# First layer: the scores of both token halves in one group on four row groups of TensorE, and a new order of the step

## What is computed

```python
def _block(x, shifted, n1g, n1b, qkvw, qkvb, pw, pb, rpb, n2g, n2b, f1w, f1b, f2w, f2b):
    shortcut = x
    x = _ln(x, n1g, n1b).reshape(B, H, W, DIM)
    if shifted:
        x = jnp.roll(x, (-SHIFT, -SHIFT), (1, 2))
    xw = _win_part(x)
    qkv = (xw @ qkvw.T + qkvb).reshape(-1, N, 3, HEADS, HD).transpose(2, 0, 3, 1, 4)
    q, k, v = (qkv[0], qkv[1], qkv[2])
    attn = jnp.einsum('bhnd,bhmd->bhnm', q * SCALE, k)
    attn = attn + rpb[RPI].transpose(2, 0, 1)[None]
    ...
    attn = jax.nn.softmax(attn, -1)
    xw = jnp.einsum('bhnm,bhmd->bnhd', attn, v).reshape(-1, N, DIM)
    xw = xw @ pw.T + pb
    ...
    h = _ln(x, n2g, n2b)
    h = jax.nn.gelu(h @ f1w.T + f1b, approximate=False) @ f2w.T + f2b
    return x + h
```

## Time and profile before

| what | value |
|---|---|
| median of the runs | 979.84 us |
| the profiled execution | 981.16 us |
| its span on the core | 979.3 us |
| PE busy (matmul), share of the span | 801.5 us, 82% |
| DVE busy | 794.5 us, 81% |
| ACT busy | 574.2 us, 59% |
| POOL busy | 237.1 us, 24% |
| the chain that ended last, by engine | PE 62%, DVE 27%, ACT 5%, issue 3% |
| 302.58 to 313.73 (one step): PE, DVE, ACT busy | 11.15, 9.78, 8.56 us |
| granted clock of TensorE, 17.6 to 52.0 and 302.58 to 313.73 | 0.65 and 1.00 |

### The profile page before, as it was taken

How to read it: one execution, slowest core, us unless ns; L and a number is a source line. 1 busy time by engine, 2 the same in 40 slices (tenths; PEclk the granted TensorE clock), 3 DMA queues, 4 the chain that set the end, 5 groups by cost and what they waited for, 6 DMA issues and landing times.

```text
span 979.3 us, 20396 instructions
## 1 busy us (share of the span) xinstructions
PE 801.5 (82%) x7980; PEld 534.8 (55%) x7980; DVE 794.5 (81%) x2001; ACT 574.2 (59%) x859; POOL 237.1 (24%) x272
## 2 busy tenths in 40 slices
PE   3799999999999999999999988799577668332366
PEld 1577877877787777777777764374211111000053
DVE  8788889988888998888899965755539999899942
ACT  1276777777777777777676663224466664645032
POOL 6122222222222222222222211382201221222021
PEclk8699999999999999999999997889676655565657
DMA  8200000000000000002000000100003665666301
GB/s 229 63 1 3 1 2 2 2 2 2 2 2 2 2 2 1 2 1 105 1 3 2 2 2 1 48 1 1 1 1 66 129 130 102 124 130 129 65 0 33
DMA packets 11621, 34.13 MB, mean 35 GB/s; under 512 B 1879, under 2 KB 4359, under 8 KB 11271
## 3 DMA queue, kind: packets, MB, share of 16 engines
q0 software_dynamic: 5904, 21.24, 11.5%
q1 hardware_dynamic: 5623, 11.60, 4.0%
HBM read 10.81 MB, written 0.79 MB: 12 GB/s over the span
## 4 chain that ended last, share of the span: by engine, by line
PE 62%; DVE 27%; ACT 5%; issue 3%; POOL 1%; DMA 1%; POOLq 0%; SPq 0%; DVEq 0%; ACTq 0%
PE narrow L1450 5%; PE wide L1373 4%; PE scores_a L1422 4%; PE scores_b L1422 4%; DVE prod L989 4%; PE last L1527 4%; DVE prod L997 3%; PE scores_a L1409 3%; PE scores_b L1433 3%; PE scores_b L1409 3%; PE scores_a L1433 3%; PE narrow L1480 3%; PE last L1523 2%; PE wide L1513 2%; PE last L1500 2%
## 5 line engine op out<-in xcount | busy, mean ns | idle before, releaser
L380 POOL TENSOR_TENSOR stb<-stb,neg_half 128x4 f32<-128x4 f32 x48 | 48.4, 1008 | 253.3 <-DVE stb L681 253.3
L1102 ACT ACTIVATE d<-d 128x768 f32<-128x768 f32 x96 | 80.6, 840 | 18.4 <-DVE d L628 17.9
L1450 PEld LDWEIGHTS narrow<-v,pt 128*64 128x64 f32 x2304 | 79.5, 139 | 13.4 <-issue 13.4
L1450 PE MATMUL narrow<-v,pt 128*64 128x54 f32 x2304 | 85.8, 225 | 0.1
L1697 PE MATMUL scores_b<-xb,gates_w 128*32 128x512 bf16 x192 | 26.0, 557 | 60.1 <-DVE yo L1009 51.4
L375 POOL TENSOR_TENSOR sta<-sta,neg_half 128x4 f32<-128x4 f32 x48 | 48.9, 1018 | 104.9 <-DVE sta L568 104.9
L1109 ACT ACTIVATE pt<-scores_a 128x768 f32<-128x768 f32 x48 | 38.9, 810 | 56.7 <-PE scores_a L1433 56.7
L1118 ACT ACT_TABLE_LOAD x47 | 60.3, 1283 | 0.8
L615 DVE TENSOR_REDUCE mx<-scores_a 128x12 f32<-128x768 f32 x48 | 46.0, 958 | 16.8 <-PE scores_a L1422 16.8
L1102 ACT ACT_TABLE_LOAD x46 | 59.0, 1283 | 0.8
L1118 ACT ACTIVATE ga<-wide 128x512 f32<-128x512 f32 x48 | 28.7, 598 | 49.6 <-PE wide L1513 49.5
(11 more groups left out here) (351 smaller groups left out, 2200.9 us busy)
## 6 DMA issues: line engine op xcount, KB each, us to landing
gsum<-mag POOLq DMA_DIRECT2D x14, 512.0 KB, 4.6
ysum<-yo POOLq DMA_DIRECT2D x7, 768.0 KB, 5.8
ysum<-xd POOLq DMA_DIRECT2D x6, 768.0 KB, 5.8
gsum<-mag POOLq DMA_DIRECT2D x14, 256.0 KB, 4.7
wts<-in_wpack SPq DMA_DIRECT2D x6, 442.0 KB, 6.7
sed_w<-in_sed_in SPq DMA_DIRECT2D x1, 2304.0 KB, 8.0
graw<-in_gates_in SPq DMA_DIRECT2D x1, 1152.0 KB, 5.1
x_all<-in_x_tok SPq DMA_DIRECT2D x8, 96.0 KB, 3.2
```

Source lines behind the costliest of these rows:

```text
L1102: act.activation(d, d, ACT.Exp).then_inc(p_ready[u], 1)
L1450: op = pe.matmul(y_ps[64 * b:64 * b + 64, q * VO:(q + 1) * VO], t.pt[:, q, h, 64 * b:64 * b + 64], t.v[:, q, b, h * VO:(h + 1) * VO], star ...
```

## The change

- `scores` takes no half any more: one call does both, after the same waits, and the order inside is v, b, r, u, so that neighbouring matmuls go to different row groups. One semaphore `pe_S` replaces two.
- The order in PE's, DVE's, ACT's and POOL's loops is new. In PE's a slot is now transposed (`windows_T`) in step n, projected and scored in n + 1, its probabilities and values in n + 2, its projection and `fc1_a` in n + 3, `fc1_b` and `fc2` in n + 4. Both `bias` calls stand together, right ahead of `windows_T` and `scores`.
- PE's and ACT's loops run one step longer, DVE's and POOL's two. The jobs tied to fixed steps at the end move by one or two steps with it.
- `gelu` is split into `gelu_a` and `gelu_b`, which stand a step apart; `gelu_b` comes first in a step, then both affine steps, then `gelu_a`.
- Waits follow the new order: `windows_T` waits for `take_v` of the slot before, `project_v` for `add_proj`, `transpose_z` for `affine_a` three slots ahead, each of them the latest reader of the bank y.

```diff
-            for k in range(SLOTS + 4):
-                if k >= 45:
-                    rstd_f(k - 45)
-                rstd_b(k - 3)
-                add_b2(k - 3)
+            for k in range(SLOTS + 6):
+                if k >= 47:
+                    rstd_f(k - 47)
+                add_b2(k - 5)
                 rstd_a(k)
                 if k == 0:
                     rstd_e(1)
                     set_values()
                     rstd_e(2)
+                rstd_b(k - 4)
...
-                        dve.wait_ge(pe_S[1], n - 1)
+                        dve.wait_ge(pe_S, n - 1)
...
-                if r == 0:
-                    dve.wait_ge(mx_ready[u], n + 1)
-                    if n >= 2:
-                        dve.wait_ge(pe_PT[1], n - 1)
+                dve.wait_ge(mx_ready[u], n + 1)
+                if n >= 2:
+                    dve.wait_ge(pe_PT[1], n - 1)
...
-            for k in range(SLOTS + 4):
-                if k >= 45:
-                    final_stats(k - 45)
-                if k == 51:
+            for k in range(SLOTS + 6):
+                if k >= 47:
+                    final_stats(k - 47)
+                if k == 53:
                     fill(4)
                     final_normal(6)
                     fill(5)
-                invert(k - 3)
-                divide(k - 3)
-                subtract(k - 2, 0, 1)
-                take_o(k - 3)
                 if k == 1:
-                    embed_centre(1)
-                normal_a(k - 1)
-                if k == 1:
+                    normal_a(0)
                     embed_square(1)
                     embed_centre(2)
                     embed_square(2)
-                add_proj(k - 3)
-                squares_b(k - 3)
-                variance_b(k - 3)
-                maxima(k - 2, 1)
-                subtract(k - 2, 1, 0)
-                subtract(k - 2, 1, 1)
-                normal_b(k - 3)
-                if k == 50:
+                    embed_finish(1)
+                squares_a(k)
+                normal_b(k - 5)
+                variance_a(k)
+                if k > 1:
+                    normal_a(k - 1)
+                maxima(k - 3, 0)
+                subtract(k - 3, 0, 1)
+                subtract(k - 3, 0, 0)
+                maxima(k - 3, 1)
+                add_mlp(k - 6)
+                subtract(k - 3, 1, 1)
+                invert(k - 4)
+                divide(k - 4)
+                subtract(k - 3, 1, 0)
+                if k == 52:
                     fill(2)
                     fill(3)
-                if k == 2:
+                take_o(k - 4)
+                take_k(k - 2)
+                add_proj(k - 4)
+                squares_b(k - 4)
+                variance_b(k - 4)
+                if k == 3:
                     dve.wait_ge(set_v, 9)
                     dve.wait_ge(set_on, 6)
-                take_v(k - 2)
-                take_k(k - 1)
-                if k == 1:
-                    embed_finish(1)
-                squares_a(k)
-                variance_a(k)
-                add_mlp(k - 4)
-                maxima(k - 1, 0)
-                subtract(k - 1, 0, 0)
-                if 45 <= k < 51:
-                    final_normal(k - 45)
+                take_v(k - 3)
+                if k == 0:
+                    embed_centre(1)
+                if 47 <= k < 53:
+                    final_normal(k - 47)
...
-            def gelu(n):
+            def gelu_a(n):
                 if live(n):
                     t = st[n % 2]
                     act.wait_ge(pe_f1a, n + 1)
                     if n >= 2:
                         act.wait_ge(pe_f2, n - 1)
                     act.activation(t.g1[:], hid_bank[:, :, 0:256], ACT.Gelu).then_inc(g1_made, 1)
+
+            def gelu_b(n):
+                if live(n):
+                    t = st[n % 2]
                     act.wait_ge(pe_f1b, n + 1)
+                    if n >= 2:
+                        act.wait_ge(pe_f2, n - 1)
                     act.activation(t.g2[:], z_ps[:, 0:256], ACT.Gelu).then_inc(g2_made, 1)
 
...
-            for k in range(SLOTS + 3):
+            for k in range(SLOTS + 4):
+                exponential(k - 2, 0)
+                take_q(k - 1)
+                exponential(k - 2, 1)
                 take_PT(k - 2, 0)
-                exponential(k - 2, 1)
-                take_q(k - 1)
-                affine_b(k - 3)
-                if k == 50:
-                    fill(3)
                 take_PT(k - 2, 1)
-                gelu(k - 3)
-                exponential(k - 1, 0)
+                gelu_b(k - 4)
                 affine_a(k)
                 if k % CHUNKS == 1 and k // CHUNKS < BLOCKS - 1:
                     table_high(k // CHUNKS + 1)
                 if k % CHUNKS == 4 and k // CHUNKS < BLOCKS - 1:
                     table_middle(k // CHUNKS + 1)
-                if k == 49:
+                affine_b(k - 3)
+                if k == 50:
                     for c in range(3):
                         fill(c)
+                gelu_a(k - 3)
                 if k == 50:
+                    fill(3)
+                if k == 51:
                     fill(4)
                     fill(5)
+
...
-                    pe.wait_ge(x1_ready, n - 1)
+                    pe.wait_ge(v_ready, n - 1)
+                elif n == 1:
+                    pe.wait_ge(xa_ready, 1)
...
-                if live(n + 1):
-                    pe.wait_ge(xa_ready, n + 2)
+                if n >= 1:
+                    pe.wait_ge(x1_ready, n)
                 else:
-                    pe.wait_ge(x1_ready, n)
+                    pe.wait_ge(xa_ready, 2)
...
-            def scores(n, u):
+            def scores(n):
                 if not live(n):
                     return
                 t = st[n % 2]
-                if u == 0:
-                    pe.wait_ge(q_ready, n + 1)
-                    pe.wait_ge(k_ready, n + 1)
+                pe.wait_ge(q_ready, n + 1)
+                pe.wait_ge(k_ready, n + 1)
                 for v in range(2):
                     for b in range(2):
                         for r in range(2):
-                            rows, cols = slice(64 * r + 32 * u, 64 * r + 32 * u + 24), slice(128 * v + 64 * b, 128 * v + 64 * b + 64)
-                            op = pe.matmul(sc_bank[u][64 * b:64 * b + 64, r, 192 * v:192 * v + 192], t.q[rows, cols], t.k[rows, :, cols],
-                                           start=False, stop=True, skip_group_check=True)
-                op.then_inc(pe_S[u], 1)
+                            for u in range(2):
+                                rows, cols = slice(64 * r + 32 * u, 64 * r + 32 * u + 24), slice(128 * v + 64 * b, 128 * v + 64 * b + 64)
+                                op = pe.matmul(sc_bank[u][64 * b:64 * b + 64, r, 192 * v:192 * v + 192], t.q[rows, cols], t.k[rows, :, cols],
+                                               start=False, stop=True, skip_group_check=True)
+                op.then_inc(pe_S, 1)
 
...
+                    else:
+                        pe.wait_ge(xa_ready, 3)
...
-                if live(n + 1):
+                if live(n + 3):
+                    pe.wait_ge(xa_ready, n + 4)
+                elif live(n + 1):
                     pe.wait_ge(v_ready, n + 2)
...
-            for k in range(SLOTS + 3):
+            for k in range(SLOTS + 4):
+                project_qk(k - 1)
+                values_T(k - 3)
+                probs_T(k - 2, 0)
+                proj(k - 3)
+                probs_T(k - 2, 1)
+                fc1_b(k - 4)
+                project_v(k - 2)
+                bias(k - 1, 0)
                 bias(k - 1, 1)
-                proj(k - 2)
-                scores(k - 1, 1)
                 windows_T(k)
+                scores(k - 1)
+                transpose_z(k - 3)
+                if k == 51:
+                    final_T(4)
+                    final_T(5)
+                    conv(0, (2,))
+                fc2(k - 4)
                 if k == 50:
-                    conv(0, (2,))
-                fc2(k - 3)
-                if k == 49:
                     pe.wait_ge(set_ypad, 1)
                     pe.wait_ge(conv_ready, 1)
                     conv(0, (0,))
-                probs_T(k - 1, 0)
-                project_v(k - 1)
-                project_qk(k)
-                bias(k, 0)
-                transpose_z(k - 2)
-                probs_T(k - 1, 1)
-                scores(k, 0)
-                values(k - 1, 0)
-                values(k - 1, 1)
-                fc1_a(k - 2)
-                fc1_b(k - 2)
-                if k == 48:
-                    final_T(0)
-                    final_T(1)
-                values_T(k - 1)
-                if k == 48:
-                    final_T(2)
-                    final_T(3)
+                fc1_a(k - 3)
+                values(k - 2, 0)
+                values(k - 2, 1)
                 if k == 49:
-                    final_T(4)
-                    final_T(5)
```

(8 more changed lines are left out.)

## The result

The changed kernel is slower: median 999.02 us (998.22 to 999.51, 4 runs) against 979.66 (976.84 to 980.69) for the kernel before, a ratio of 1.0201, 95% interval 1.0181 to 1.022. Forecast were 950.3 and, at most, 971. The profiled execution took 998.53, its span 996.7 against 979.3.

A forecast was written before the change was run, and what follows sets the result against it. TensorE (PE) was taken to bound the first layer's steady step, 11.15 us. Steady part -31.4, start +2.5, end -0.6 sum to -29.5 us: profiled 981.16 to 951.7, median 950.3, range 941 to 971.

The forecast's parts named there:

- behind the layer: Everything after the first layer: taken as untouched by the change, so no term in the sum.
- Part 1, the score group: Both score halves on PE overlap across row groups: 0.84 us instead of twice 0.81, saving 0.78 us a step.
- Part 2, the plain step: First layer's steady step in the new order: PE stays fed, 10.37 us plus 0.08 for waits, 10.45 against 11.15.
- The sensitive margins before `probs_T`: PE reaches `probs_T(a)` 0.03 us and `probs_T(b)` 0.10 us after their exp results are ready, so no wait on paper.
- rival C: A wait on the chain `fc1_a`, Gelu, table load, exp(a) costs 0.3 us more a step: 964 us; chance 15%.
- B: Rival: the score group is bound by weight loads, 1.13 us instead of 0.84, 13 us less gain: 963; chance 17%.
- D: Rival: the halves' row groups do not overlap, scores cost 1.62 us, the kernel gets slower: 985 us; chance 10%.
- Part 2, the longer steps: Shifted blocks and table and weight jobs at block turns: extra time stays 17.6 us in all, bounds 12 and 24.
- The sentence on what would be wrong altogether: PE waiting for DVE in every step would mean DVE's queue was mislaid, a loop of 11 us instead of 9.5.
- Part 3: Start and end of the first layer: +2.5 us at the start (bounds 0 and +7), -0.6 at the end (give or take 3).
- Rival E: Better than forecast: no loss at the start and DVE absorbs the table jobs, 941 us; chance 5%.

The follow-up runs named there:

- Experiment 4: The kernel of Experiment 1 with the two score halves as separate groups and `windows_T` between them; 979.5 us, ratio 1.0011 to the kernel before.
- Experiment 1: The changed kernel with DVE's two table jobs (`table_rest`, `table_low`) one step later in DVE's loop; 957.2 us, ratio 0.9769 to the kernel before.
- Experiment 2: The changed kernel with 36, 14 or 8 unread matmuls ahead of `transpose_z` in the nine long steps, waits kept; 976.1 us, ratio 0.9944.
- experiment 6: The kernel of Experiment 5 with eight sign jobs of a later stage moved from DVE's steps 40 to 47 to 51 to 53; 945.89 us, ratio 0.9659.
- Experiment 5: The kernel of Experiment 1 with DVE's first two fills behind `normal_b(47)` instead of ahead of it; 954.55 us, ratio 0.9746.
- experiment 8: The kernel of experiment 6 with table jobs spread in pieces, plus slot 47's MLP ahead of the first convolution; 946.89 us, ratio 0.9659.
- experiment 3: The kernel of Experiment 1 with the score matmuls half by half, 16 of a, then 16 of b; 958.49 us, ratio 0.979.

## Why the prediction was wrong

The terms of the sum, forecast against measured in the profiled executions: the 45 plain steps 470.3 against 45 x 10.47 = 471.2 (+0.9); the longer steps 17.6 against 60.5 (+42.9); the start +2.5 against -1.2 (-3.7); the end -0.6 against +4.1 (+4.7); behind the layer 0 against +2.1. Together 46.9 on 951.7: 998.6, measured 998.53.

- **Part 1, the score group: right.** Forecast 0.84, recorded 0.87 (0.84 on the chain), in four bursts of eight. Experiment 4 shows by separating the halves that this overlap is the whole gain of the plain step. The Trainium skill's price of a load (TensorE: Matmul & The Clock Gate, LDWEIGHTS), by which 32 of them would take 1.7 us, is not what the trace shows (0.87).
- **Part 2, the plain step: right in the mechanism,** 10.45 forecast, 10.45 to 10.48 measured, no engine waited for. That the number fits to the hundredth is luck: 0.08 of it stood there for waits, and the trace has none, PE's pieces add up to 10.45 themselves (`transpose_z` 0.37 where the sum had 0.22, `project_qk` 1.05 for 0.89, against shorter `proj` and `fc1_b`). The sensitive margins before `probs_T` held, so rival C has nothing in it, and B and D fell with the 0.87.
- **Part 2, the longer steps: this step failed, and with it the sign.** The prediction wrote that they "keep their cause" and bounded them by 12 and 24. It named both new places, ACT's copies ahead of `affine_b` and DVE's jobs after `take_v`, and took each for some extra length of its own queue. That one of them waits for the other, and which one runs first in real time, was not asked. DVE's loop runs one step ahead of ACT's: the step of DVE whose tail meets ACT's `affine_a` of step k is step k + 1. With the jobs in steps 2 and 5 on DVE and 1 and 4 on ACT of each eight, they meet in the same moment. Experiment 1 shows this: 40.0 of the 42.9 us go with one step's delay, and the longer steps cost 20.5 where the sum had 17.6.
- **The price of a wait on PE: missing altogether.** The bounds counted waits as waits. Experiment 2 shows that 24.2 of the 40.0 us are the lower clock behind them, about as much as the 24.9 us of the nine waits themselves.
- **The sentence on what would be wrong altogether** named the right pair, PE waiting for DVE, but for every step and for another reason (DVE's length). It came in nine steps and from ACT by way of DVE. DVE's length sets nothing in a plain step; it does in steps 40 to 47 (experiment 6).
- **Part 3.** The start was mis-sized: not a loss of 2.5 but a gain of 1.2. The prediction had let the steps there run at the low clock; from 0 to 64 us the granted clock is 0.99 after and 0.81 before. Why it stays up there was not tested. The end was mis-sized by 4.7: the values of slot 47 take 2.98 (lower clock), PE then stands 4.76 for `normal_b(47)`, and the first convolution starts 28.7 us after the scores of slot 47 where it had started 25.7. Experiment 5 shows that this wait is in the path to the last add (16.25 and 16.27 us from its end to that add), and that the clock ahead of it is too; experiment 8, that moving the last slot's MLP forward only puts the convolution off. How the 4.7 us divide among these was not tested.
- **Behind the layer,** +2.1 us in untouched code (374.15 against 372.03). Over the profiled executions of all kernels this stretch lies between 370.0 and 374.2, so the 2.1 need not come from the change. The granted clock from 33 to 93 us behind the last add is 0.84 after and 0.87 before; what sets it was not tested.

Experiment 1, with that one cause away, gives 957.2, inside the range of 941 to 971. Its terms against the sum are +0.9 for the plain steps, +2.9 for the longer ones, -4.2 at the start, +4.5 at the end and +1.8 behind the layer. That it lies this near is in part luck: the errors at the start and at the end cancel. Rival E's 941 should have been 942.2 by its own terms (950.3 - 2.5 - 5.6), which changes nothing. None of the rivals, whose chances added up to 1, was a rare job that meets its producer.

## What to carry to other kernels

When loops of several engines are reordered, list every rare job that one engine hands to another and compute for each the real time of both ends, not only the place in its own queue; a loop that runs a step ahead turns a margin of 6 us into a wait. Price a wait on TensorE by two numbers: its length and the work that follows at the lower clock. Matmuls that used different row groups overlapped here when they were neighbours in the queue, so put them next to each other; the order among them made no difference; and once the bound engine is faster, spread long side jobs in pieces.

## What the runs showed of the hardware

- Matmuls of different row groups are recorded as starting out of program order: in experiment 3 half b's first burst starts 0.06 us behind half a's first, although a's other 12 stand ahead of it, and the group takes 0.87 us as with interleaving by hand (298.68 to 299.55).
- 32 recorded f32 matmuls of 24 rows in four row groups cost 0.87 us when they are neighbours, 16 in two row groups 0.81; with two transposes between the halves it is 0.81 and 0.82 (experiment 4).
- A wait of 1.35 us on PE was followed by values that took 2.73 and 3.06 instead of 1.77 us (steps 8 and 24 of the changed kernel), the same as after one of 4.66. In experiment 1 a wait of 1.05 us at the same place of the step was followed by values of 1.77, 2.84 and 3.07 us (steps 4, 20, 36), so its length alone does not say whether the clock falls. With PE kept busy up to 0.63 us before its next group the level stayed at 2.4 GHz.
